# Issuing the third part of an attention unit's transposes behind the next score

## The reference

```
q, k, v = proj(Wq, bq), proj(Wk, bk), proj(Wv, bv)
scores = einsum('bhqd,bhkd->bhqk', q, k) / sqrt(D)
scores = where(causal, -inf, scores) + alibi_bias(S)
probs = softmax(scores, axis=-1)
out = einsum('bhqk,bhkd->bhqd', probs, v)
return out.transpose(0, 2, 1, 3).reshape(B, S, E) @ Wo.T + bo
```

## Time and profile before

| | |
|---|---|
| median of 3 runs | 1640.9 us (1637.94 to 1645.32) |
| the profiled execution | 1637.66 us, its span 1635.9 us |
| PE busy, share of the span | 1479.2 us, 90% |
| DVE, ACT, POOL busy | 1047.6, 888.6, 567.1 us |
| mean granted TensorE clock | 0.976 |
| attention, from the first score to the last transposes | 57 to 1171 us of the span |
| the experts | 1171 us to the end |

### The profile page before, as it was taken

The page is one execution under the profiler, slowest core; times in us unless marked ns, Lnnn a source line. Parts: engine busy times, 40 slices in busy tenths (PEclk is TensorE's granted clock), DMA queues, the critical chain, the costliest instruction groups (busy, mean ns, idle before and its releaser), DMA issues.

```text
span 1635.9 us, 35508 instructions
## 1 busy us (share of the span) xinstructions
PE 1479.2 (90%) x12763; PEld 889.9 (54%) x12763; DVE 1047.6 (64%) x2485; ACT 888.6 (54%) x2029; POOL 567.1 (35%) x595
## 2 busy tenths in 40 slices
PE   3799988998998899989799898999889999999995
PEld 1465555655555555655455466565356656566563
DVE  6688787666778767777878877777334333333331
ACT  4477776665777666676766565667312222222221
POOL 3111132121113222112311134231215777777775
PEclk9899999999999999999999899999989999999998
DMA  6244431433423243542324241324687888788783
GB/s 254 74 131 114 123 91 58 112 104 101 118 90 96 88 136 115 149 128 76 97 64 116 77 115 52 87 78 164 220 260 110 136 129 141 129 140 136 127 145 45
DMA packets 171350, 193.28 MB, mean 118 GB/s; under 512 B 87536, under 2 KB 121072, under 8 KB 171056
## 3 DMA queue, kind: packets, MB, share of 16 engines
q1 hardware_dynamic: 143760, 151.67, 34.3%
q0 software_dynamic: 26128, 37.24, 13.7%
q10 hardware_dynamic: 1296, 2.11, 0.3%
HBM read 93.45 MB, written 53.74 MB: 90 GB/s over the span
## 4 chain that ended last, share of the span: by engine, by line
PE 67%; DVE 11%; issue 7%; ACT 5%; DMA 4%; SPq 4%; POOL 2%; DVEq 0%; POOLq 0%; ACTq 0%
PE S L1175 15%; PE T L1098 11%; PE O L1114 7%; PE S L1055 5%; PE S L1087 5%; PE O L1206 4%; PE M L1206 4%; PE M L1055 4%; DVE arena L1480 4%; SPq L932 3%; PE S L1072 2%; PE M L1137 2%; PE M L1072 2%; ACT arena L1670 2%; DVE arena L1491 1%
## 5 line engine op out<-in xcount | busy, mean ns | idle before, releaser
L1480 DVE CUSTOM_DVE_ANT_0 arena<-S,cF,nsl 128x1024 f32<-128x1024 f32 (+7 forms) x512 | 413.2, 811 | 60.0 <-PE S L1087 56.9
L1098 PE MATMUL T<-cF,arena 128*128 128x128 f32 x2304 | 368.1, 281 | 77.4 <-ACT arena L1684 42.6
L1670 ACT ACTIVATE arena<-arena,mneg 128x1024 f32<-128x1024 f32 (+7 forms) x512 | 395.4, 772 | 47.8 <-DVE mneg L1480 46.8
L1684 ACT ACTIVATE arena<-T 128x512 f32<-128x512 f32 (+3 forms) x544 | 241.8, 457 | 276.3 <-PE T L1098 274.2
L1098 PEld LDWEIGHTS T<-cF,arena 128*128 128x128 f32 x2304 | 267.9, 142 | 179.2 <-ACT arena L1684 47.8
L1175 PE MATMUL S<-arena 128*128 x1704 | 270.4, 316 | 8.9 <-issue 8.9
L1823 POOL DMA_INDIRECT out<-arena x142 | 222.1, 1564 | 106.8 <-ACT arena L1730 53.7
L1491 DVE COPY arena<-T 128x512 f32<-128x512 f32 (+3 forms) x288 | 153.6, 536 | 138.8 <-PE T L1098 137.0
L1175 PEld LDWEIGHTS S<-arena 128*128 128x128 f16 x1704 | 167.9, 99 | 108.4 <-issue 10.3
L1114 PE MATMUL O<-arena 128*32 128x128 f32 (+1 forms) x3328 | 211.3, 330 | 8.3 <-DVE arena L1511 7.1
L1087 PE MATMUL S<-arena 96*128 96x512 f16 (+3 forms) x768 | 213.1, 332 | 3.8 <-DMA arena<-arena 2.5
(11 more groups left out here) (187 smaller groups left out, 1822.3 us busy)
## 6 DMA issues: line engine op xcount, KB each, us to landing
arena<-arena SPq DMA_DIRECT2D x192, 128.0 KB, 2.4
arena<-in_w1T SPq DMA_DIRECT2D x64, 352.0 KB, 3.5
arena<-in_x SPq DMA_DIRECT2D x64, 256.0 KB, 3.4
w_d<-arena SPq DMA_DIRECT2D x32, 352.0 KB, 2.9
arena<-w_d SPq DMA_DIRECT2D x16, 704.0 KB, 7.2
arena<-in_w2T SPq DMA_DIRECT2D x32, 256.0 KB, 2.9
out<-arena SPq DMA_DIRECT2D x32, 256.0 KB, 3.2
xn_d<-arena SPq DMA_DIRECT2D x24, 256.0 KB, 2.0
```

The source lines that it names most:

```text
L1098: tp = pe.transpose(z[:, (c - c0) * P:(c - c0 + 1) * P], ring[u % 4][:, c * P:(c + 1) * P], idf)
L1480: dve.tensor_tensor_reduce(ring[r][:, 0:w], SBK[o.bank["score", u]][:, 0:w], rel[:, S - w:S], nsl[:, hh:hh + 1], 3.0e38, ALU.add, ALU.min, ...
L1670: act.activation(ring[r][:, 0:w], ring[r][:, 0:w], ACT.Exp, bias=mneg[:, m:m + 1], scale=-1.0, accum_out=rs[:, k, c:c + 1]).then_inc(sems[ ...
L1684: act.activation(PT[k][:, h, to_:to_ + gap * (c1 - c0 - 1) + 1:gap, :], TB[o.bank["tr", u, i]][:, 0:n].rearrange("p (c n) -> p c n", n=P), ...
```

## The change

`turned` becomes a generator that issues either the first two parts or the third. In turn u the first two parts of unit u-4 stand where all of them stood. The third part's transpose stands behind `score` of unit u, and its copy behind `mx` of unit u. Units with one or two parts are issued as before. Since `lighter` is asked for the third copy at a later point, its choices change for 136 of the 832 copies; in total 8 copies go from ACT to DVE (ACT then has 201, 130, 99 and 106 copies of 4, 3, 2 and 1 blocks of 128 columns, DVE 119, 62, 29 and 86), and of the 64 third copies DVE now has 51 where it had 33.

```
     def score(u):
         o.take("S", "score", u)
         add("score", u)
+        late = turned(u - LAG, True) if u >= LAG else iter(())
+        next(late, None)
         add("mx", u)
+        for _ in late:
+            pass
         o.leave("S", ("score", u), ("mx", u))
...
-    def turned(u):
+    def turned(u, late):
+
         for i, (c0, c1, at, gap) in enumerate(turn_parts(u)):
+            if (i > 1) != late:
+                continue
             o.take("T", "tr", u, i)
             add("tr", u, i)
+            yield
             en = lighter((c1 - c0) * P)
             add("pt", u, i, en, sem="pt" + en)
...
-        if u % 8 == 7:
+        if u % 8 == 7 and not late:
             add("rx", u)
...
         if 0 <= u - LAG < NU:
-            turned(u - LAG)
+            for _ in turned(u - LAG, False):
+                pass
+            if u >= NU:
+                for _ in turned(u - LAG, True):
+                    pass
```

## The result

The changed kernel takes 1621.53 us, the median of 4 runs (1617.62 to 1624.22), against 1640.12 for the kernel before on the same chip (also 4 runs): a ratio of 0.988 with a 95% interval of 0.9853 to 0.9906. Run again later beside other kernels it gave 0.9879 (0.9851 to 0.9907). Ratios here are the recorded estimates; they can differ by 0.1 to 0.2% from the quotient of the two medians given with them.

A forecast was written before the change was run, and what follows sets the result against it. PE was taken to set the pace, stopping where a T bank is not yet emptied. Terms -18.0 + 1.9 + 4.5 = -11.6 us put the profiled execution at 1626.1 and the median at 1629 us, range 1618 to 1639.

The forecast's parts named there:

- more is won: Rival: `pv` follows at 0.11 and ACT's earlier `exp` shortens later waits; 22 us kept whole, 1619 us; chance 0.12.
- The pace: Attention: PE sets the pace; its idle column, 25.4 us ahead of the 64 third parts, understates the stops.
- The transpose behind the score: At the 64 third parts the score hides the wait for the first copy (37 short, 23 long); 18.0 us saved.
- the 0.11 bound: Third transpose to `pv`: 0.11 us as lower limit instead of the chosen 0.20; would save 5.8 us more.
- the idle column's price of 10 us in all: Third parts: saving if summed from printed PE idle time, capped at a score's length, instead of start-to-start times.
- `mx` behind the third transpose: `mx` of unit u waits for the third transpose of u-4, which ends no later than before; cost nothing.
- The copy behind `mx`: Third copy frees its bank later, delaying the next large unit's first part at 11 places; 1.9 us charged, 0 to 6.3.
- `exp` no longer behind the copy: ACT is freed 0.28 us earlier at up to 31 places; counted as nothing, gain at most 8.7 us.
- The deal of the copies: 136 copies change engine between ACT and DVE; nothing in sum, 3 to 4 us either way.
- Kept to the end: PE time saved is partly lost where PE only meets its next wait earlier; a quarter, 4.5 us, taken off.
- most is lost again: Rival: stops shortened at third parts are made up at later waits; a third of 18 us kept, 1637 us; chance 0.2.
- the bank as the wait: Rival: the late third copy stops PE two turns on, 26 us lost against 18 won; 1649 us; chance 0.05.

The follow-up runs named there:

- order_only: Changed kernel, but with every copy on the engine it had in the kernel before; 1622.16 us, 0.9909 of the kernel before.
- pv_first: Changed kernel with third transpose, `mx` and third copy also moved behind the piece of `pv` that follows the score; 1629.64 us, 0.9945 of before.
- all_last: Changed kernel with the last part of every large unit, not only a third one, behind the score; 1627.94 us, 0.9935 of before.
- copy_first: Changed kernel, same copy engines, with the third copy ahead of `mx` and the transpose still behind the score; 1617.9 us, 0.9888 of before.
- half: Changed kernel, same copy engines, with the third part late for only two of a block's four large units; 1624.86 us, 0.9928 of before.
- copy_only: Kernel before with only the third copy moved behind `mx`, on the changed kernel's copy engines; 1640.23 us, 1.0018 of before.
- two_banks: Kernel before's order, the three parts of large units with j = 6 put into two banks; 1605.07 us, 0.9821 of before; repeated 1607.0 us.

## Why the prediction was right

The forecast was 1629 us, from 11.6 us of gain; 18.6 came, within the range of 1618 to 1639 and on its faster side. The time lies nearer to the rival *more is won* (1619) than to the forecast, but not by that rival's reasons: `pv` followed at 0.203 and not at 0.11, and no run shows a gain from an earlier `exp`. The mechanism was right, the size came out low. Step by step:

- *The pace.* PE sets it, and the idle column understates its stops. Right: at the 64 places the idle column fell by 10.9 us, and the time from the second part's last transpose to `pv` by 20.5.
- *The transpose behind the score.* At 37 short places 0.25 us each, 9.3 in all, were expected; 9.9 were found, 27 of them 0.253 to 0.259 and the ten others 0.295 to 0.325. The chosen 0.20 for `pv` behind a transpose was measured at 0.203, so neither the 0.11 bound nor the idle column's price of 10 us in all holds. At the 23 long places 8.3 were expected and 9.7 found, with single places between -0.4 and 1.5 as ACT's and DVE's bursts fell otherwise. The 4 others gave 1.0 and not 0.4. The whole is 20.5 against 18.0 (19.1 in order_only, with the old deal).
- *`mx` behind the third transpose* was counted as nothing. No run isolates it; the gain of order_only leaves little room for a cost. Moved further back, in pv_first and all_last, `mx` waits longer for transposes and the kernel is slower; how much of that is `mx` is open.
- *The copy behind `mx`.* 1.9 us were charged, within 0 and 6.3, and 5.1 us of new idle time stand in the trace, at 8 places where about ten were foretold and by the mechanism foretold; over copy_first it is 3.7 us. But copy_first is no faster, within the 5 us that the intervals leave. I had priced the late bank and not what its alternative costs, a copy ahead of `mx`. Whether the two cancel, or the cost is only too small for these intervals, is open.
- *`exp` no longer behind the copy* was counted as nothing, and copy_first agrees: it puts `exp` behind the copy again and is no slower.
- *The deal of the copies* was counted as nothing, 3 to 4 us either way: it gave 3 us, between none and 5.7. That part of the gain was luck as far as the forecast goes.
- *Kept to the end.* This is the term that was off: a quarter, 4.5 us, was taken off for waits that only move. The traces speak for no loss: in the change 20.5 us won at the 64 places and 5.1 lost ahead of first parts leave 15.4, and the attention is 17.3 us shorter; in order_only 19.1 less 2.9 leave 16.2, and 15 came; in half it was 8.4 and 8.8. Each of these alone, with an interval of some 4 us either way, would still allow for a quarter lost; that all three come out so makes it unlikely. With no quarter the sum is 16.1, and with the deal's 3 us 19.1.

Of the other rivals, *most is lost again* is refuted by the time itself, and the bank as the wait is real but small here; all_last shows it larger, with 10.8 us ahead of the first parts of j = 7.

The clock stands in no term of the prediction. It did not matter for the change, but between kernels a few microseconds apart it does, as copy_only and pv_first show.

## What to carry to other kernels

Measure a pipelined engine's stop from start to start and against an unhindered place of the same sequence: here a stop of 0.25 to 0.3 us, 37 times, showed as 0.04 to 0.11 us of idle time. Between two uses of the same buffer in an in-order stream put work that needs neither, as much as the wait is long. Going further back did not pay in either kernel that tried: it also moves what waits for the step (`mx`) or holds its buffer (the copy). Before hiding a wait look whether it can be taken away: packing three parts into two banks gave 12 us more than hiding the third one's wait. And before a difference of a few microseconds is given to an edit, compare the mean granted clock of the runs.

## What the runs showed of the hardware

I had not expected how exact the start-to-start distances on PE are where the granted clock is at its upper level (medians over the attention of the traces before and after). Behind a transpose the next one or a score starts 0.109 us later, and a wait adds 0.055 to the first step behind it (0.165). A score of 768 columns takes 0.328 until the next transpose and one of 896 takes 0.381. The first `pv` matmul comes 0.203 behind a transpose. So a `pv` costs 0.09 more than a transpose would in its place, behind a score (0.420 against 0.328) as behind a transpose (0.203 against 0.109); the 0.203 could be summed from pairs that stand in the kernel before.

In the stretches at the lower level, 1.2 GHz, two transposes start 0.213 apart and not 0.109. Such stretches differ from run to run of the same kernel: the six runs of the changed kernel beside two_banks have mean granted clocks from 0.972 to 0.977.
